# Graph, attention and expert layer: the linear term moved into the mix steps, a routing stage with four slots of loads

## What is computed

```python
# _L0_gnn_ref
h = x @ weight_l
agg = segment_sum(edge_val[:, None] * h[edge_col], edge_row)
out = agg + bias_l + x @ weight_r + bias_r
# _L0_mix_ref
return out * gate @ Wproj + bproj
# together
x = x + gnn(xn, ...) + mix(xn, ...)
# _L0_ffn_ref, on the normalised x
logits = xn @ Wr + br
top_vals, top_idx = top_k(logits, 2)
```

## Time and profile before

| | us |
|---|---|
| median of 3 runs (lowest, highest) | 5057.96 (5052.91, 5059.99) |
| profiled execution, its own time | 5066.14 |
| span of its trace | 5064.2 |

### The profile page before, as it was taken

One profiled execution on the slowest core, in us unless ns is written; L12 is line 12 of the kernel. 1 busy time (PEld: TensorE's weight loads), 2 busy tenths in 40 slices (PEclk: granted clock), 3 DMA queues, 4 the chain that ended last, 5 costly groups with the idle time before them and its releaser, 6 DMA issues. The chain is left out here.

```text
span 5064.2 us, 84566 instructions
## 1 busy us (share of the span) xinstructions
PE 3791.3 (75%) x16502; PEld 2994.5 (59%) x16634; DVE 2295.8 (45%) x10289; ACT 1245.6 (25%) x2628; POOL 3300.9 (65%) x2297
## 2 busy tenths in 40 slices
PE   4777777777777777777777777764888849999995
PEld 3555555555555555555555555542555528888885
DVE  4444444444444445555555555542656641222221
ACT  1222222222222222222222222221011003444442
POOL 1336888888888888888888888885444423444442
PEclk9998888888888888888888888876555559999998
DMA  6996777777777777777777777767656655666666
GB/s 196 340 319 92 97 98 98 96 99 96 98 95 99 96 100 104 105 105 109 104 105 106 108 104 105 107 81 159 207 194 199 198 146 135 142 145 145 142 142 182
DMA packets 644846, 683.19 MB, mean 135 GB/s; under 512 B 65384, under 2 KB 599364, under 8 KB 644546
## 3 DMA queue, kind: packets, MB, share of 16 engines
q0 software_dynamic: 293040, 312.13, 46.2%
q1 hardware_dynamic: 338178, 361.33, 23.5%
q10 hardware_dynamic: 13584, 9.24, 0.7%
HBM read 280.99 MB, written 414.27 MB: 137 GB/s over the span
## 5 line engine op out<-in xcount | busy, mean ns | idle before, releaser
L818 POOL DMA_INDIRECT agg<-msg,sidx x1664 | 2580.4, 1551 | 541.0 <-issue 376.7
L1016 PE MATMUL bank<-rows,Cmat 128*128 (+1 forms) x3328 | 1032.5, 448 | 167.1 <-ACT msg L1166 164.4
L1166 ACT COPY msg<-bank 128x512 f32<-128x512 f32 x832 | 487.0, 585 | 2250.4 <-DMA agg<-msg,sidx 1963.0
L1016 PEld LDWEIGHTS bank<-rows,Cmat 128*128 128x128 f32 x3328 | 686.1, 223 | 391.3 <-issue 303.5
L883 DVE SCALAR_TENSOR_TENSOR sidx<-seen_sum,trash,srcf 128x4 int32<-128x4 f32 x416 | 92.6, 223 | 1458.6 <-DMA agg<-msg,sidx 1458.4
L1895 POOL DMA_INDIRECT x_rows_and_trash<-x_y,x_node x224 | 345.1, 1541 | 547.5 <-DVE x_y L1879 497.8
L1001 PE MATMUL bank<-Emat,pick 128*128 128x128 f32 x3328 | 545.2, 317 | 195.1 <-DVE seen L870 192.4
L866 DVE TENSOR_SCALAR Emat<-bank,srcf,wtf 128x128 f32<-128x128 f32 x1664 | 565.0, 399 | 0.0
L1001 PEld LDWEIGHTS bank<-Emat,pick 128*128 128x128 f32 x3328 | 516.9, 229 | 51.3 <-issue 17.0
L870 DVE SCALAR_TENSOR_TENSOR seen<-bank,srcf,prior 128x128 f32<-128x128 f32 x1664 | 479.7, 342 | 0.0
L1808 PE MATMUL bank<-x_xf,x_w 128*128 128x256 f32 x1792 | 407.5, 381 | 1.3 <-ACT x_xf L1836 1.3
(11 more groups left out here) (243 smaller groups left out, 4153.4 us busy)
## 6 DMA issues: line engine op xcount, KB each, us to landing
x_w<-in_L_ffn_W_dram SPq DMA_DIRECT2D x112, 512.0 KB, 4.9
agg<-zeros SPq DMA_DIRECT2D x196, 256.0 KB, 5.1
r_agg<-agg SPq DMA_DIRECT2D x196, 256.0 KB, 4.4
x_zin<-expert_table SPq DMA_DIRECT2D x112, 259.0 KB, 5.1
rows<-h_rows SPq DMA_DIRECT2D x208, 128.0 KB, 2.8
agg<-msg,sidx POOLq DMA_INDIRECT x1664, 3.8
xn_rows<-xnr POOLq DMA_DIRECT2D x49, 256.0 KB, 4.7
xn_turned<-xnT POOLq DMA_DIRECT2D x49, 256.0 KB, 4.9
```

The source lines that it names most:

```text
L818: pool.indirect_dma_start(scratch["agg"][r][:, :], bass.IndirectOffsetOnAxis(ap=sidx[:, j:j + 1], axis=0), msg[:, j % (2 * BATCH), :], Non ...
L1016: mm = nc.tensor.matmul(M[p][:, (q % 2) * D:(q % 2 + 1) * D], Cmat[:, b % 2, q, :], rows[:, bass.ds(slot, 1), :], start=True, stop=True)
L1166: nc.scalar.copy(msg[:, at:at + 2, :].rearrange("p q c -> p (q c)"), M[p][:, :]).then_inc(s_msg, 1)
```

## The change

The linear term and the three biases leave the routing stage: their weights are loaded at the start of the edge stage, and `project` adds three more products to each of its two accumulations. The routing stage then loads five tiles per pair, into one of four slots, with the load of pair i+4 issued when pair i has been summed. The accumulators 2 and 3 are summed by PE (`sum_rest`, two products with the identity into a PSUM bank, L1519) and no longer by POOL, so DVE adds three times. `route` and `position` follow two pairs late, in another order within the round. The bias of the logits is added by DVE in place of two products. The send semaphores are one per half and table.

```diff
+DEPTH = 4
...
+                   (wr[:], halves(t["L0_gnn_weight_r"])), (brows[:, 0, :], row(t["L0_gnn_bias_l"])),
+                   (brows[:, 1, :], row(t["L0_gnn_bias_r"])), (brows[:, 2, :], row(t["L0_mix_bproj"]))]
...
+            nc.vector.tensor_tensor(bsum[:], brows[:, 0, :], brows[:, 1, :], ALU.add).then_inc(s_bias, 1)
+            dve.wait_ge(s_bias, 1)
+            nc.vector.tensor_tensor(bsum[:], bsum[:], brows[:, 2, :], ALU.add).then_inc(s_bias, 1)
...
                 for a in range(HALF):
-                    mm = nc.tensor.matmul(bank, oT[:, a, s * P:(s + 1) * P], wproj[:, a, :], start=(a == 0),
-                                          stop=(a == HALF - 1))
+                    nc.tensor.matmul(bank, oT[:, a, s * P:(s + 1) * P], wproj[:, a, :], start=(a == 0), stop=False)
+                for a in range(HALF):
+                    nc.tensor.matmul(bank, xT[:, u, s, a, :], wr[:, a, :], start=False, stop=False)
+                mm = nc.tensor.matmul(bank, ones[0:1, :], bsum[:], start=False, stop=True)
                 if s == 1:
                     mm.then_inc(s_p, 1)
...
+def over_fours(engine, body):
+
+    for i in range(2 * DEPTH):
+        body(i, i % DEPTH)
+    with engine.Fori(2, PAIRS // DEPTH) as k:
+        for u in range(DEPTH):
+            body(DEPTH * k + u, u)
+    for i in range(PAIRS // DEPTH * DEPTH, PAIRS):
+        body(i, i % DEPTH)
...
-        xin = sb("r_xin", [P, 2, 2, D])
-        agg = [sb(f"r_agg{r}", [P, 2, 2, D]) for r in range(NACC)]
-        half = sb("r_half", [P, 2, 2, D])
+        xin = sb("r_xin", [P, DEPTH, 2, D])
+        agg = [sb(f"r_agg{r}", [P, DEPTH, 2, D]) for r in range(NACC)]
...
-            def load(k, s):
-                i = 2 * k + s
-                if not first(k):
-                    sp.wait_ge(s_sum, 4 * i - 4)
-                    sp.nop(nofuse=True)
-                sp.dma_start(xT[:, s].rearrange("p c a r -> p c (a r)"), pair_of(scratch["xnT"], i)).then_inc(s_ldT[s], 16)
-                sp.dma_start(xin[:, s], pair_of(scratch["x1"], i)).then_inc(s_ld[s], 16)
-                for r in range(NACC):
-                    sp.dma_start(agg[r][:, s], pair_of(scratch["agg"][r], i)).then_inc((s_ld if r < 2 else s_ld2)[s], 16)
...
+            def load(i, u):
+                sp.dma_start(agg[2][:, u], pair_of(scratch["agg"][2], i)).then_inc(s_ld2[u], 16)
+                sp.dma_start(agg[3][:, u], pair_of(scratch["agg"][3], i)).then_inc(s_ld2[u], 16)
+                sp.dma_start(xin[:, u], pair_of(scratch["x1"], i)).then_inc(s_ld[u], 16)
+                sp.dma_start(agg[0][:, u], pair_of(scratch["agg"][0], i)).then_inc(s_ld[u], 16)
+                sp.dma_start(agg[1][:, u], pair_of(scratch["agg"][1], i)).then_inc(s_ld[u], 16)
...
+            def body(i, u, more=True):
+                sp.wait_ge(s_sum, 3 * i + 3)
                 sp.nop(nofuse=True)
-                sp.dma_start(pair_of(scratch["x1"], 2 * k + s), x1[:, s]).then_inc(s_x1st[s], 16)
...
-
+                sp.dma_start(pair_of(scratch["x1"], i), x1[:, u % 2]).then_inc(s_x1st[u % 2], 16)
+                if more:
+                    load(i + DEPTH, u)
+
+            for u in range(DEPTH):
+                load(u, u)
             for f in range(FILLS):
                 sp.dma_start(scratch["x1"][NPAD + f * CAP:NPAD + (f + 1) * CAP, :].rearrange("(a p) d -> p a d", p=P),
...
-            def add_half(k, s):
-                i = 2 * k + s
-                pool.wait_ge(s_ld2[s], 32 * k + 32)
-                if not first(k):
-                    pool.wait_ge(s_sum, 4 * i - 4)
-                nc.gpsimd.tensor_tensor(half[:, s], agg[2][:, s], agg[3][:, s], ALU.add).then_inc(s_half, 1)
...
-                i = 2 * k + s
+            def send(i, u):
                 pool.wait_ge(s_pos, 5 * i + 5)
                 for c in range(2):
                     for m in range(2):
-                        if not (first(k) and s == 0 and c == 0):
-                            pool.wait_ge(s_sent[m], 16 * (2 * i + c))
+                        if not below(i, 1):
+                            pool.wait_ge(s_sent[c][m], 16 * i)
                         pool.nop(nofuse=True)
                         pool.indirect_dma_start(scratch["table"][m][:, :],
-                                                bass.IndirectOffsetOnAxis(ap=pos[:, s, c, m:m + 1], axis=0),
-                                                z[:, s, c, :], None).then_inc(s_sent[m], 16)
-            add_half(0, 0)
...
+            def gather_sums(i, u):
+                x = x1[:, u % 2]
+                dve.wait_ge(s_ld[u], 48 * visits(i, u) + 48)
+                if not below(i, 2):
...
-                nc.vector.tensor_tensor(x1[:, s], xin[:, s], agg[0][:, s], ALU.add).then_inc(s_sum, 1)
-                dve.wait_ge(s_sum, 4 * i + 1)
-                nc.vector.tensor_tensor(x1[:, s], x1[:, s], agg[1][:, s], ALU.add).then_inc(s_sum, 1)
-                dve.wait_ge(s_sum, 4 * i + 2)
-                dve.wait_ge(s_half, i + 1)
-                nc.vector.tensor_tensor(x1[:, s], x1[:, s], half[:, s], ALU.add).then_inc(s_sum, 1)
-                dve.wait_ge(s_sum, 4 * i + 3)
-                dve.wait_ge(s_lin, i + 1)
-                flat = x1[:, s].rearrange("p c d -> p (c d)")
-                nc.vector.tensor_tensor(flat, flat, LIN[s][:, :], ALU.add).then_inc(s_sum, 1)
-
-            def statistics(k, s):
...
+                    dve.wait_ge(s_x1st[u % 2], 16 * ((i - u % 2) // 2))
+                nc.vector.tensor_tensor(x, xin[:, u], agg[0][:, u], ALU.add).then_inc(s_sum, 1)
+                dve.wait_ge(s_sum, 3 * i + 1)
+                nc.vector.tensor_tensor(x, x, agg[1][:, u], ALU.add).then_inc(s_sum, 1)
+                dve.wait_ge(s_sum, 3 * i + 2)
+                dve.wait_ge(s_rest, i + 1)
+                flat = x.rearrange("p c d -> p (c d)")
+                nc.vector.tensor_tensor(flat, flat, REST[u % 2][:, :], ALU.add).then_inc(s_sum, 1)
...
-                if not first(k):
-                    dve.wait_ge(s_T, i - 1)
-                    dve.wait_ge(s_sent[0], 16 * (2 * i - 2))
-                    dve.wait_ge(s_sent[1], 16 * (2 * i - 2))
-                nc.vector.tensor_copy(z[:, s, :, D], nodes[:, bass.ds(2 * i, 2)])
+                if not below(i, DEPTH):
+                    dve.wait_ge(s_T, i - DEPTH + 1)
+                    for c in range(2):
+                        for m in range(2):
+                            dve.wait_ge(s_sent[c][m], 16 * (i - DEPTH + 1))
...
-                nc.vector.tensor_copy(lg[:], L[s][:, 0:2 * NE].rearrange("p (a e) -> p a e", a=2)).then_inc(s_lg, 1)
+                nc.vector.tensor_tensor(lg[:], logit, br[:].rearrange("p (a e) -> p a e", a=1).to_broadcast([P, 2, NE]),
+                                        ALU.add).then_inc(s_lg, 1)
...
-            def body(k, s):
-                gather_sums(k, s)
-                statistics(k, s)
-                if not (first(k) and s == 0):
-                    route(*before(k, s))
-                    position(*before(k, s))
-                normalise(k, s)
-
-            over_pairs(dve, body)
-            route(*divmod(PAIRS - 1, 2))
-            position(*divmod(PAIRS - 1, 2))
+            def body(i, u):
+                old = None if below(i, 2) else (i - 2, (u - 2) % DEPTH)
+                if old:
+                    route(*old)
+                gather_sums(i, u)
+                statistics(i, u)
+                if old:
+                    position(*old)
+                normalise(i, u)
+
+            over_fours(dve, body)
+            for i in range(PAIRS - 2, PAIRS):
+                route(i, i % DEPTH)
+                position(i, i % DEPTH)
 
         @block.tensor
         def _(pe):
-            pe.wait_ge(s_w, 128)
+            pe.wait_ge(s_w, 16 * 4)
             pe.wait_ge(s_bits, 1)
-            pe.wait_ge(s_bias, 2)
-
...
+            def sum_rest(i, u):
+                pe.wait_ge(s_ld2[u], 32 * visits(i, u) + 32)
+                if not below(i, 2):
+                    pe.wait_ge(s_sum, 3 * i - 3)
+                for r in (2, 3):
+                    mm = nc.tensor.matmul(REST[u % 2][:, :], ident[:], agg[r][:, u].rearrange("p c d -> p (c d)"),
+                                          start=(r == 2), stop=(r == 3))
+                mm.then_inc(s_rest, 1)
...
-                        nc.tensor.matmul(bank, xf[:, s, a, c * P:(c + 1) * P], wrt[:, a, :], start=(a == 0), stop=False)
-                    mm = nc.tensor.matmul(bank, ones[0:1, :], br[:], start=False, stop=True)
+                        mm = nc.tensor.matmul(bank, xf[:, s, a, c * P:(c + 1) * P], wrt[:, a, :], start=(a == 0),
+                                              stop=(a == HALF - 1))
...
-            def body(k, s):
-                more = not (isinstance(k, int) and 2 * k + s == PAIRS - 1)
-                after = (k, 1) if s == 0 else (k + 1, 0)
-                if not (first(k) and s == 0):
-                    rank(*before(k, s))
-
-                if more:
```

(54 more changed lines are left out.)

132 lines of the change are left out of this document (57 added, 75 removed).

## The result

The changed kernel takes **4948.68 us** (median of 4 runs, 4946.66 to 4949.62), before it in the same comparison 5058.98 us (4 runs, 5052.91 to 5060.96). The ratio is 0.9784, 95% interval 0.977 to 0.9798. That is 110 us less; the forecast was 83 less, at 4975, with a range of 4900 to 5015.

The account below looks back on a forecast made before the run. POOL's transfers bound the edge stage and a ring of waits the routing stage. Savings of 78 (rounds), 3 (start) and 5 (end), less 3 (edge start), make 83 us: 5057.96 to 4975 us, range 4900 to 5015.

Parts of the forecast that it names:

- the forecast's own case: Routing stage: a round of 10.0 to 10.6 us, giving a total of 4959 to 4991 us; chance 0.63.
- rival 1: Routing stage: PE's clock rises, a warm round takes 8.6 us, total 4898, about 4935 if half warm; chance 0.17.
- The ring: Routing stage: ranks, PE's `sum_rest`, third sum, statistics, position, scaling, next `route`, ranks again; turn and logits fall out.
- The round's size: Routing stage: seven terms sum to 10.26 us a round against 11.92 before; 47 rounds save 78 us.
- that line and gap: DVE in the routing round: L1438 at 0.17 us without POOL's half sum, plus 0.05 to the next start.
- L1438 beside POOL: Routing stage, DVE: this line takes 0.53 us beside POOL's half sum, 0.17 without it.
- Start and end: Routing stage: 3 us less to first ranks, 5 less at its end; edge stage's start 3 us more.
- The later first root: Routing stage's start: ACT's first square root left at its time, though shared queues could make it up to 5 us later.
- Mix steps at 0: Edge stage: six more products per pair, 2.6 us warm or 5.1 cold, lie under POOL's time and cost 0.
- Another wait in the ring's place (2): Routing stage: sends or loads fill the freed time, round 11.4 us, total 5029; chance 0.11.
- The mix steps got no slower (3): Denies rival: edge stage's mix steps slow, cold PE adding 5.1 us per pair, total 5225 if fully uncovered; chance 0.05.

Follow-up runs that it names:

- e1: Changed kernel with `sum_rest(i)` issued ahead of turn(i-1) and the ranks of i-2 on PE, not behind them: 4839.04 us, ratio 0.9556.
- e2: Changed kernel with accumulators 2 and 3 summed by POOL in SBUF as before, PE summing nothing: 4901.94 us, ratio 0.9682.
- e7: e1 plus an idle POOL sum of a constant tile once per pair, which nothing reads: 4893.25 us, ratio 0.9664.
- e4: Changed kernel with `project`'s four products by wr issued twice in the mix steps: 4952.3 us, ratio 0.9783.
- e8: e1 with all four accumulators summed by PE and one DVE addition in place of three: 4832.32 us, ratio 0.9538.
- e3: Kernel before with only the linear term and its biases moved to the mix steps: 4991.99 us, ratio 0.9858.
- e5: Changed kernel with two load slots in place of four, z keeping four: 4954.54 us, ratio 0.9784.
- e6: e1 with two load slots in place of four: 4834.85 us, ratio 0.9546.
- e9: e1 with routing one pair late instead of two: 4903.04 us, ratio 0.9693.
- e10: e6 with ACT's 24 expert weight transfers issued three each behind the roots of pairs 0 to 7: 4827.57 us, ratio 0.9545.
- e11: e8 with the expert weight transfers issued behind the roots of the first eight pairs: 4808.64 us, ratio 0.9503.

## Why the prediction was right, and where it was off

- **The number.** 4949 is in the range but under the forecast's own case, 4959 to 4991 (a round of 10.0 us gives 4963 by its terms, not 4959), in the part that was kept open for rival 1. It is not that rival: the mechanism is the forecast's own, and its round was sized too long.
- **The ring.** Right: DVE waits for `sum_rest` and nothing else of size (61.7 us in 300 named so, and 19.1 more at the same sum), and e1 shows that the ring, not an engine, set the round.
- **The round's size.** 10.26 forecast, 9.74 measured; 47 x 0.52 = 24 of the 27 us missed. By term, means over 47 rounds: ranks 0.18 (forecast 0.24), `sum_rest` 3.75 (3.89), third sum to statistics 0.72 (0.72), to the line that was L1438 1.14 (1.14), that line and gap 0.08 (0.22), position to the end of the scaling 2.18 (2.36), `route` to ranks 1.69 (1.69). Two terms were counted as duration plus a gap, where the next instruction starts before the last is written as ended: L1479 starts 0.08 us after L1429's start, not 0.22. In the round shown `route` starts 2.24 us after position's start. In `sum_rest`, 3.80 is typical, and every eighth round has 3.4. The other 3 us are less than the rows of the table that the change does not explain.
- **L1438 beside POOL.** Right: 0.17 with no half sum. e2 and e7 show what it can cost: 0.36 us in the round shown of the kernel before, but 1.28 as soon as DVE is the bound. The change gave up this cost for a larger one: with POOL's sum (e2) the half sum's 1.3 us are in the round, but the 3.75 of `sum_rest` are not, and the kernel is 47 us faster than the changed one.
- **Start and end.** First ranks -3.7 (forecast -3), end -3.7 (-5), edge stage's start +2.0 (+3). The later first root, +2.8, was named as up to 5.
- **Mix steps at 0.** Right: e4 doubles most of the added products and the ratio stays (0.9783, 0.9784).
- **Rivals.** The clock (1) rose from 0.53 to 0.59 only, and every eighth round's shorter `sum_rest` makes 0.05 us of a round; in e8, with twice the products, it did rise. Another wait in the ring's place (2) didn't come. The mix steps got no slower (3): POOL's waits for messages were 6.1 us, before 7.4.
- **Parts of the change.** The prediction took the change as a whole. The runs say: linear term moved -69 us (e3), then lag of two pairs, slots and the logits' bias together -90 (e2), then TensorE's sums at their place **+47**. The 90 are not divided further. The two extra load slots are worth nothing beside TensorE's sums (e5, e6), and the lag alone is worth 64 where those sums lie ahead (e9); neither was tried on e2 itself.

## What to carry over

When no engine is full, write down the ring of waits and ask of each link whether it must stand in it: the sums on PE had their operands early and sat in the ring only because they were issued behind an instruction that waits. Work moved to an idle engine can cost more than it frees; here it paid only once it was issued first. A POOL sum on SBUF cost DVE its full duration where DVE was the bound (1.28 and 1.05 us a round), and 0.36 us of 1.28 in the round shown of the kernel before. And when a wait is removed and the time stays, look at what stands in the queue behind it: in e10 and e11 15 transfers of zeros stand there, which the stage needs only at its end; what moving them is worth no run shows.

## What the runs showed of the hardware

- A DVE operation of 128x2 elements took 1.47 us beside a POOL sum of 1.27 us and 1.25 beside one of 1.05, against 0.17 alone.
- The granted clock of the routing stage was 0.53 with PE busy 84% of the time in the kernel before, 0.59 at 64% in the changed one, 0.94 at 83% in e8's window: in these runs a higher busy share does not go with a higher clock. What sets it, they don't show.
- The two fp32 products of `sum_rest`, 512 columns each and four records, took 3.76 us at the lower level and 1.96 at the upper (e1, start to end), so that `sum_rest` is half as long where the clock is granted.
- At the start of e10's routing stage no compute engine was full and the DMA share was 1.00 for 60 us. There a first root that came 21.7 us earlier than in e6 left DVE 11.5 us ahead at the third pair and 5.4 at the last.
